# Causal attention in a fused adaLN, attention and MoE kernel: the columns above the diagonal block are no longer computed

## The reference, cut to what matters

```
h = layernorm(x) * (1 + ca) + sa                 # ca, sa: per batch and channel, from L0_c @ L0_wmod
q, k, v = einsum('bsd,hed->bhse', h, W_Q / W_K / W_V)
scores = einsum('bhse,bhme->bhsm', q, k) / sqrt(128)
scores = where(key position > query position, -1e9, scores)      # causal
z = softmax(scores) @ v
x = x + ga * einsum('bhse,hde->bsd', z, W_O)
h = layernorm(x) * (1 + cb) + sb
x = x + gb * ffn(h)
```

## Time and profile before

| what | us |
|---|---|
| the profiled execution, own time | 4296.39 |
| its span on the slowest core (core 6) | 4294.9 |
| spans of the 8 cores | 4263.1 to 4294.9 |
| two timed runs | 4277.14 and 4645.7, median 4461.42 |
| TensorE busy, core 6 | 3511.9 (82% of the span) |
| VectorE busy | 1183.2 (28%) |
| ScalarE busy | 672.9 (16%) |

### The profile page before, as it was taken

One profiled execution on the slowest core, in us unless ns is written; L12 is line 12 of the kernel. 1 busy time (PEld: TensorE's weight loads), 2 busy tenths in 40 slices (PEclk: granted clock), 3 DMA queues, 4 the chain that ended last, 5 costly groups with the idle time before them and its releaser, 6 DMA issues. The chain is left out here.

```text
span 4294.9 us, 46986 instructions; the slowest of 8 cores (4263.1 to 4294.9 us)
## 1 busy us (share of the span) xinstructions
PE 3511.9 (82%) x14133; PEld 1375.2 (32%) x14394; DVE 1183.2 (28%) x2423; ACT 672.9 (16%) x1120; POOL 469.0 (11%) x891
## 2 busy tenths in 40 slices
PE   3544488888888888888889349999999999999997
PEld 1222222222222222222224214444444444444443
DVE  0144422222222222222222631221222212212222
ACT  0233222222222222222220310000000000000000
POOL 1101000000000000000001002121221211212211
PEclk8666677777767766777769669999999999999998
DMA  9877410100001010101004006454455454544544
GB/s 209 148 144 145 80 18 15 16 15 15 14 12 15 15 15 15 15 15 15 15 15 64 10 10 91 67 75 73 74 77 74 72 81 72 79 69 74 79 70 117
DMA packets 128933, 246.57 MB, mean 57 GB/s; under 512 B 15681, under 2 KB 56770, under 8 KB 126402
## 3 DMA queue, kind: packets, MB, share of 16 engines
q0 software_dynamic: 125824, 209.92, 32.4%
q1 hardware_dynamic: 2882, 33.63, 2.3%
HBM read 444.94 MB, written 8.39 MB: 106 GB/s over the span
## 5 line engine op out<-in xcount | busy, mean ns | idle before, releaser
L543 PE MATMUL pacc<-h_full,rA 128*128 128x512 bf16 x2497 | 616.7, 405 | 23.6 <-DMA rA<-wk 17.1
L1226 PE MATMUL pdn<-ysb,rD 128*128 128x512 bf16 x2510 | 566.6, 386 | 15.5 <-DVE ysb L1170 9.8
L1116 PE MATMUL px<-h,rA 128*128 128x512 bf16 x2508 | 564.8, 380 | 3.9 <-ACT comb L329 1.2
L1141 PE MATMUL px<-h,rA 128*128 128x512 bf16 x2508 | 562.2, 379 | 2.7
L543 PEld LDWEIGHTS pacc<-h_full,rA 128*128 128x128 bf16 x2560 | 261.8, 103 | 364.4 <-issue 128.0
L1158 DVE TENSOR_TENSOR ysb<-x1s,px 128x1024 bf16<-128x1024 bf16 x80 | 97.7, 1221 | 961.2 <-PE px L1141 961.2
L1226 PEld LDWEIGHTS pdn<-ysb,rD 128*128 128x128 bf16 x2560 | 253.5, 99 | 327.6 <-issue 36.6
L1116 PEld LDWEIGHTS px<-h,rA 128*128 128x128 bf16 x2560 | 251.0, 98 | 305.1 <-issue 4.8
L1141 PEld LDWEIGHTS px<-h,rA 128*128 128x128 bf16 x2560 | 250.5, 98 | 302.1
L1236 DVE SCALAR_TENSOR_TENSOR x_own<-pdn,gbcl,x_own 128x512 f32<-128x512 f32 x320 | 240.2, 751 | 346.0 <-PE pdn L1226 346.0
L1130 ACT ACTIVATE x1s<-px 128x1024 bf16<-128x1024 f32 x80 | 81.9, 1023 | 1480.2 <-PE px L1116 1480.1
(11 more groups left out here) (149 smaller groups left out, 2445.5 us busy)
## 6 DMA issues: line engine op xcount, KB each, us to landing
rB<-wmodA POOLq DMA_DIRECT2D x96, 512.0 KB, 9.5
rA<-wg POOLq DMA_DIRECT2D x128, 256.0 KB, 4.9
rA<-wu POOLq DMA_DIRECT2D x128, 256.0 KB, 5.0
rD<-wd POOLq DMA_DIRECT2D x256, 128.0 KB, 5.5
xl<-ximg SPq DMA_DIRECT2D x16, 1024.0 KB, 11.8
rA<-wk POOLq DMA_DIRECT2D x32, 256.0 KB, 4.7
rA<-wq POOLq DMA_DIRECT2D x32, 256.0 KB, 4.7
rA<-wv POOLq DMA_DIRECT2D x32, 256.0 KB, 4.7
```

The lines of the kernel that those rows point to most:

```text
L543: t.matmul(pacc[:, bank * 512:bank * 512 + 512], ub[:, (dc % 8) * 128:(dc % 8) * 128 + 128], moving_fn(dc, qtr), start=(dc == 0), stop=(dc ...
L1116: lambda t, ub=ub, dc=dc, half=half: t.matmul(px1[:, half * 512:half * 512 + 512], ub[:, (dc % 8) * 128:(dc % 8) * 128 + 128], h2[:, dc * ...
L1141: lambda t, ub=ub, dc=dc, half=half: t.matmul(px3[:, half * 512:half * 512 + 512], ub[:, (dc % 8) * 128:(dc % 8) * 128 + 128], h2[:, dc * ...
L1226: t.matmul(pdn[rot][:, :], ub[:, dloc * 128:dloc * 128 + 128], ysb[:, hc * 1024 + th * 512: hc * 1024 + th * 512 + 512], start=(hc == 0), ...
```

## The change

Each pair gets an offset `q0`, the first query column that it needs: 0 for pairs up to the diagonal's first tile, then 128, 256 and 384. So F1, F2, F3, B1, B2, B3 and F5' to F7', B5' to B7' become 384, 256 and 128 columns wide. The exponential is split into two instructions, one for each key tile, in every pair, since the two halves are no longer adjacent. The memsets are gone. No wait and no semaphore is otherwise moved.

```diff
+        def q0_of(tc):
+            li = max(0, tc // 2 - 4 * grp)
+            return li * 128
+        q0a, q0b = q0_of(tca), q0_of(tcb)
...
-        for k in range(2):
+        for k, q0 in ((0, q0a), (1, q0b)):
             em.op("tensor",
-                  lambda t, k=k, ptens=ptens, negm_row=negm_row: t.matmul(
-                      ptens[:, k * 512:k * 512 + 512], ones_row_bf[:, :], negm_row,
-                      start=True, stop=False),
+                  lambda t, k=k, q0=q0, ptens=ptens, negm_row=negm_row: t.matmul(
+                      ptens[:, k * 512 + q0:k * 512 + 512], ones_row_bf[:, :],
+                      negm_row[0:1, q0:512], start=True, stop=False),
                   waits=w_st if k == 0 else (), inc=False)
...
+                      q_sb[:, grp * 512 + q0:grp * 512 + 512], start=False, stop=True),
                   waits=(), inc=(k == 1))
...
-        s_exp = em.op("scalar",
-                      lambda s, ptb=ptb, ptens=ptens: s.activation(ptb[:, :], ptens[:, :],
-                                                                   AF.Exp),
-                      waits=w_exp, inc=True)
+        em.op("scalar",
+              lambda s, ptb=ptb, ptens=ptens, q0=q0a: s.activation(
+                  ptb[:, q0:512], ptens[:, q0:512], AF.Exp),
+              waits=w_exp, inc=(q0b >= 512))
+        if q0b < 512:
+            em.op("scalar",
+                  lambda s, ptb=ptb, ptens=ptens, q0=q0b: s.activation(
+                      ptb[:, 512 + q0:1024], ptens[:, 512 + q0:1024], AF.Exp),
+                  inc=True)
+        s_exp = em.mark("scalar")
...
-                elif tc > 2 * l + 1:
-                    last_dep = em.op("vector",
-                                     lambda v, ptb=ptb, c0=c0: v.memset(
-                                         ptb[:, c0:c0 + 128], 0.0),
-                                     waits=[s_exp], inc=True)
-                    em.drain("vector")
...
-                      plr[0:1, 0:512], ones_bf[:, :], ptb[:, k * 512:k * 512 + 512],
+                      plr[0:1, q0:512], ones_bf[:, :],
+                      ptb[:, k * 512 + q0:k * 512 + 512],
...
-                      pz[:, :], vtok[:, tc * 128:tc * 128 + 128],
-                      ptb[:, k * 512:k * 512 + 512],
+                      pz[:, q0:512], vtok[:, tc * 128:tc * 128 + 128],
+                      ptb[:, k * 512 + q0:k * 512 + 512],
```

More of the change, by code:

```diff
@@ L633, in emit_pair_front @@
             w_st += [g["pacc"][0], g["pacc"][1]]
-        for k in range(2):
+        for k, q0 in ((0, q0a), (1, q0b)):
             em.op("tensor",
-                  lambda t, k=k, ptens=ptens, negm_row=negm_row: t.matmul(
-                      ptens[:, k * 512:k * 512 + 512], ones_row_bf[:, :], negm_row,
-                      start=True, stop=False),
+                  lambda t, k=k, q0=q0, ptens=ptens, negm_row=negm_row: t.matmul(
+                      ptens[:, k * 512 + q0:k * 512 + 512], ones_row_bf[:, :],
+                      negm_row[0:1, q0:512], start=True, stop=False),
                   waits=w_st if k == 0 else (), inc=False)
-        for k, tc in ((0, tca), (1, tcb)):
+        for k, tc, q0 in ((0, tca, q0a), (1, tcb, q0b)):
             em.op("tensor",
-                  lambda t, tc=tc, k=k, ptens=ptens, grp=grp: t.matmul(
-                      ptens[:, k * 512:k * 512 + 512], k_sb[:, tc * 128:tc * 128 + 128],
-                      q_sb[:, grp * 512:grp * 512 + 512], start=False, stop=True),
+                  lambda t, tc=tc, k=k, q0=q0, ptens=ptens, grp=grp: t.matmul(
+                      ptens[:, k * 512 + q0:k * 512 + 512],
+                      k_sb[:, tc * 128:tc * 128 + 128],
+                      q_sb[:, grp * 512 + q0:grp * 512 + 512], start=False, stop=True),
                   waits=(), inc=(k == 1))
@@ L676, in emit_pair_front @@
                     em.drain("vector")
-                elif tc > 2 * l + 1:
-                    last_dep = em.op("vector",
-                                     lambda v, ptb=ptb, c0=c0: v.memset(
-                                         ptb[:, c0:c0 + 128], 0.0),
-                                     waits=[s_exp], inc=True)
-                    em.drain("vector")
-        return (p, pti, ptb, last_dep, tca, tcb)
+        return (p, pti, ptb, last_dep, tca, tcb, q0a, q0b)
     def emit_pair_back(ctx, R, vtok_done):
-        (p, pti, ptb, last_dep, tca, tcb) = ctx
+        (p, pti, ptb, last_dep, tca, tcb, q0a, q0b) = ctx
+        grp_off = {}
         w_l = [last_dep]
@@ L690, in emit_pair_back @@
                 w_l.append(g["plr"])
-        for k in range(2):
+        first = True
+        for k, q0 in ((0, q0a), (1, q0b)):
+            if q0 >= 512:
+                continue
             em.op("tensor",
-                  lambda t, ptb=ptb, k=k, p=p, R=R: t.matmul(
-                      plr[0:1, 0:512], ones_bf[:, :], ptb[:, k * 512:k * 512 + 512],
+                  lambda t, ptb=ptb, k=k, q0=q0, p=p, R=R: t.matmul(
+                      plr[0:1, q0:512], ones_bf[:, :],
+                      ptb[:, k * 512 + q0:k * 512 + 512],
                       start=(p == 0 and k == 0), stop=(p == R // 2 - 1 and k == 1)),
-                  waits=w_l if k == 0 else (), inc=(k == 1))
+                  waits=w_l if first else (), inc=(k == 1))
+            first = False
         w_av = []
@@ L701, in emit_pair_back @@
                 w_av.append(g["pz"])
-        for k, tc in ((0, tca), (1, tcb)):
+        first = True
+        for k, tc, q0 in ((0, tca, q0a), (1, tcb, q0b)):
+            if q0 >= 512:
+                continue
             em.op("tensor",
-                  lambda t, ptb=ptb, k=k, tc=tc, p=p, R=R: t.matmul(
-                      pz[:, :], vtok[:, tc * 128:tc * 128 + 128],
-                      ptb[:, k * 512:k * 512 + 512],
+                  lambda t, ptb=ptb, k=k, tc=tc, q0=q0, p=p, R=R: t.matmul(
+                      pz[:, q0:512], vtok[:, tc * 128:tc * 128 + 128],
+                      ptb[:, k * 512 + q0:k * 512 + 512],
                       start=(p == 0 and k == 0), stop=(p == R // 2 - 1 and k == 1)),
-                  waits=w_av if k == 0 else (), inc=(k == 1))
+                  waits=w_av if first else (), inc=(k == 1))
+            first = False
         t_av = em.mark("tensor")
@@ L852, in build_nc @@
             for p in range(R // 2):
[L853 removed]
+                ctx = emit_pair_front(h, grp, R, p, nrow, s_ng, vt_last)
                 pend_q.append((grp, R, nrow, ctx))
```

## The result

| | before | after |
|---|---|---|
| profiled execution, slowest core's span | 4294.9 | 4145.6 |
| timed runs, median | 4299.45 (10 runs) | 4147.24 (11 runs) |

The ratio of after to before is 0.9671, with a 95% interval from 0.965 to 0.9691: 3.3% faster, about 140 us. The medians also hold disturbed runs, in which some cores show a lower clock and take longer; the ratios leave these out, and where too few runs are left for a ratio the fastest run stands for it. The fastest runs of the two kernels, 4277.1 and 4145.6, are 132 us apart. The forecast was 2.9% (-126 us), with 4170 from the profiled execution and 4151 from a run of 4277. The changed kernel took 4147.

What follows compares the result with a forecast made beforehand. The pair stage was taken as limited by columns streamed through PE, mostly at the half clock (1.2 GHz). -133 - 6 + 6 + 2 + 5 = -126 us, from 4296.4 to 4170 (4151 from 4277); 8-in-10 range 4120 to 4230.

Steps and rivals of the forecast that it cites:

- Term 1: Pair stages: narrowed blocks stream fewer columns, 8.3 us a head, 133 us less for 16 heads (bounds 82 and 164).
- first trio: Fronts F1 to F3 of the pair stage, at the half clock: narrowing saves 2.56 us a head.
- Term 2: Pair stages: without 384 memsets on DVE the last backs' 7.4 us wait for masks goes; -6 us (0 to -7).
- Term 3: Exponential in two: F3 waits for ACT in F0 to F3, 0.35 us a head, +6 us (2 to 9).
- fast release: F3's wait for ACT if ACT releases PE in 0.11 us rather than 0.56: 0.14 us.
- Term 4: B7' and sometimes F7' at full clock: weight loads of 128-column matmuls partly uncovered; +2 us (0 to +38).
- Term 5: Pair-stage clock afterwards: +14 us from full clock lost after B0, -9 from an earlier rise; together +5 (-26 to +44).
- second trio: Backs B1 to B3: narrowing saves 1.28 us in five heads, 2.35 in eleven, 2.0 a head.
- first kind of head: Five of 16 heads, pair-stage clock 0.67, B1 to B3 at full clock; expected to become like the others, about +14 us.
- first rival: Narrower work leaves PE at 1.2 GHz in all of the pair stage: 4211, or about 4220 us; chance 0.13.
- (second): Pair stages: narrow matmuls don't shrink with their columns, 4206 us; chance 0.10.
- (third): K projections after the pair stage stay slow longer; 4405 us with 70 more slow matmuls a head; chance 0.03.

Runs made afterwards that it cites:

- e8: Kernel before with the fronts' first matmul given 128 rows (all but one zeros) in place of one, nothing narrowed; fastest run 4099.0 us.
- e6: Changed kernel with the fronts' first matmul given 128 rows (all but one zeros) in place of one; ratio to the kernel before 0.938, fastest run 4002.4 us.
- e4: Changed kernel with the memsets put back, on columns that nothing reads; fastest run 4181.8 us (0.977 of the kernel before).
- e10: Changed kernel with the memsets put back, a second time; ratio to the kernel before 0.9781, runs of 4183.0 to 4189.9 us.
- e1: Kernel before with each exponential split in two halves of 512 columns, nothing narrowed, memsets kept; ratio to the kernel before 1.0007.
- e5: Changed kernel with one exponential for each pair again; ratio to the kernel before 0.9693, fastest run 4144.6 us.
- e9: Changed kernel with 128-row front matmuls and one exponential, then the reciprocal's broadcast removed by 128 columns of ones; ratio to the kernel before 0.8919, fastest 3817.0 us.
- e3: Changed kernel with fronts at full width and one exponential, so only backs narrowed and memsets gone; ratio to the kernel before 0.9843.

## Why the prediction was right, step by step

**The sum and the direction** were right: -126 against about -140 (ratio 0.967), and pair stages of 45.4 us where I gave 45 to 46. The mechanism was right as well, columns that PE no longer streams. The parts were less right than their sum, and that the sum of the pair stages is within 2 us (124.4 against 126) is in part luck, as terms 1 and 5 show.

**Term 1, columns.** The price at the half clock held: F1 at 1.50 and F3 at 0.62 us (1.49 and 0.64 given), and e8 against e6 agrees with the lower price at the higher clock. The first trio gave 5.79 - 3.36 = 2.43 us a head. But the second gave nothing. From the first front of group 1 to the broadcast of group 0 the fourth and the fifth head of before took 10.6 and 14.1 us and the changed head 13.1. First the two ends of it in the fourth head of before, then in the changed head:

```profile
904.35 0.59 PE L636 MATMUL pstp<-rowbf,ones_row_bf 1*128 1x512 bf16 x2 [1.30 <-DVE pt L679]
914.95 0.58 PE L326 MATMUL pacc<-rowbf,ones_row_bf 1*128 1x512 bf16 x1 [3.09 <-DVE rowbf L788]
...
885.67 1.01 PE L640 MATMUL pstp<-rowbf,ones_row_bf 1*128 1x512 bf16 x2 [1.30 <-ACT rowbf L863]
898.81 0.58 PE L326 MATMUL pacc<-rowbf,ones_row_bf 1*128 1x512 bf16 x1 [2.23 <-DVE rowbf L803]
```

Over the 16 heads of the two cores shown the means are 13.2 us before and after, so the narrower work just about paid for the lost clock. The stretch from that broadcast to the end of the last back fell from 21.8 to 16.3, more than my 2.4 + 1.35.

**Term 2, memsets.** The 7.4 us wait went as said. The step that was mis-sized is the value of removing the memsets: I priced it by the wait in the kernel before (6 us), where backs of full width cover most of the chain. Beside narrow backs the same memsets cost 36 to 41 us (e4, e10). The sum wasn't hurt, since both edits come together, but anyone who takes the narrowing alone loses that.

**Term 3, the split.** A wait of F3 of 0.17 us in the head shown (1.24 - 1.07), against 0.14 for the fast release. Nothing measurable in all (e1, e5), where I took +6.

**Term 4, narrow matmuls at the full clock.** F7' at 1808.14 takes 0.43 us, which is 4 x 0.053 + 0.22: nothing is uncovered, where I took +2 and allowed 38. (My own figures gave +3: 0.05 us for 4 matmuls in 16 heads.) The Trainium skill's figure ("TensorE: Matmul & The Clock Gate", Back-to-back issue gap), about 81 ns for a load and matmul at 128 columns, is not what the runs show at the full clock: e9 has four in 0.22 us (904.67 to 904.89) with loads of 128x128, 55 ns each.

**Term 5, the clock.** Both halves pointed the right way and both were too small. The second trio lost to the clock all that its columns should have brought, 2.0 us a head or 32 in all, where I took +14. From the broadcast to the last back the gain of 5.5 us a head is 1.3 above the columns (3.75) and the wait for the memsets (0.5), some 20 us where I took -9. That these two errors cancel for the most part, and that term 3 cost nothing, is luck. I let five heads lose their full-clock stretch after B0; all heads of the core shown lost it, those too in which it had lasted one back. And in five heads the rise before the last backs came much sooner than the third of a block that I allowed: they have the last fronts at full clock already, and stages of 43.1 to 43.5 us. What failed is the assumption that the first kind of head turns into the second.

**Outside the stage** I forecast a few us and there were 27 in the profiled pair, about 11 of which belong to two stretches of before. For the rest, the K projection's slow start has shortened behind most heads (0.70 over 5.1 us). Why is open. It is not that the last fronts and backs run at the full clock: the five stages with 0.62 are followed by stretches of 54.7 to 54.9 us that start at 0.50, as long as those of before, and those with 0.57 by 53.3 to 53.8. So what a head gains by an early rise of the clock it gives back in part behind the same 4.2 us wait.

**The rivals.** The clock took some 12 us of the columns' gain back in the pair stages, far from the 40 of the first rival; narrow matmuls shrank with their columns (second), and the projections got a little faster, not slower (third).

## What to carry to other kernels

Skip masked columns by narrowing every operation that carries them, and drop the clears together with it, since a clear that was hidden beside wide matmuls is not hidden beside narrow ones. Before counting columns, look at the granted clock of the stretch: here a column cost half as much once PE ran at full clock (1.71 us for four matmuls of 512 columns against 0.86), and giving a one-row matmul 128 rows brought as much (143 us) as the whole change. Then look at the longest wait of PE behind a dense stretch. In this kernel it cost its own 4.2 us a head, and the matmuls behind it began at a clock of 0.50 to 0.75.

## What the runs showed of the hardware that I had not expected

- A PE that is busy without a gap can stay at the half clock: 901.0 to 913.7, 12.69 of 12.70 us busy, clock 0.50. With 128 rows, all but one of them zeros, in the place of a single row the same stage runs at 0.78 to 0.84.
- Each change between matmuls with one row or one output column and full ones cost about 0.11 us at either clock (a block of 1.93 in place of 1.71, of 1.07 in place of 0.86). With all of them full it is gone (0.86 measured in e9).
- The same instructions took 45.2 or 51.4 us from head to head (e3), with nothing but the clock between them. A part's gain read from one head is off by up to 6 us.
- The gains of two halves of an edit did not add up (154 to 158 us against 134 for both, all by fastest runs), and each half moved the clock.
- Behind the same 4.2 us wait the K projection of the changed kernel began at 0.50 in the heads whose last fronts had run at the full clock (pair stages at 0.62), and at 0.70 to 0.74 in those whose clock rose only in the backs (0.57). An early rise was not all gain.
